# Moving activation loads and spills from ScalarE's DMA queue to GpSimd's in an FFN-attention-FFN kernel on eight cores

## The chip, the cores and the metric

The kernel runs as one program on all 8 cores of one Trainium2 chip. The metric is the device time in microseconds of the slowest core. The cores share no data: each works on its own 2048 tokens of one of four sequences, and recomputes the tokens at the border that its neighbours own.

## What is computed

The reference is one layer of the "macaron" form over x of shape (4, 4096, 1024), in f32:

```python
x = x + 0.5 * ffn(layernorm(x))
x = x + attention(layernorm(x))
x = x + 0.5 * ffn(layernorm(x))
```

`ffn` is a channel mix over neighbouring tokens with three 1024 by 1024 weights, and `attention` has 16 heads of 64 channels, rotary positions and a window of 128 tokens to each side:

```python
x_prev = shift_by_one_token(x)
xr = mu_r * x + (1 - mu_r) * x_prev
xk = mu_k * x + (1 - mu_k) * x_prev
out = sigmoid(xr @ W_r.T) * (square(relu(xk @ W_k.T)) @ W_v.T)
```

## The kernel before

A core works on 20 tiles of 128 tokens (16 of them are its output, the rest is border). The residual x of a tile is f32, 128 by 1024, or 512 KB; it lives in one of eight slots of `xr_sb` (tile number modulo 8) while a tile is in work, and in the DRAM tensor `xscr` between the stages. The three stages follow one another:

- Stage 1, the first FFN (`emit_ffn_stage(1, ...)`): tiles are loaded from the input, normalised in pairs (two passes of ScalarE with sums, L203 and L206, small VectorE steps, L210 to L217, logarithm and exponential on ScalarE, L226 and L227, and L233 on VectorE), transposed by DMA on SyncE's queue, mixed on VectorE (L332, L337, L342), multiplied by W_r and W_k (L364), by W_v (L396), added to x (L409), and written to `xscr`.
- Attention (`emit_attn_stage`): for tile j it computes q, k and v (`emit_qkv`, matmuls L593, bias L598, evacuation by ScalarE L617, into PSUM banks 0 and 1 in turn), then the LayerNorm of tile j + 1 (`emit_ln2`), the attention core of tile j - 2 (scores L696, exponential L705 on ScalarE, gates L710, values L723), and the output projection of tile j - 3 (`emit_wo`, L776, bias L781, added to x by VectorE at L787). Then the finished x of tile j - 3 is written to `xscr`, and tile j + 5 is loaded into the same slot.
- Stage 4, the second FFN: as stage 1, with a border tile ahead (its LayerNorm and transpose into `lnb`), and 16 tiles that go to `out`.

The weights share one SBUF tensor, `warena`, with four columns of 1024: three for the stage's weights and one for the output projection. At start GpSimd's queue loads it with a cast from f32 to f16. During stage 1 the same queue converts the qkv weights into `wqkv16` in DRAM, and at j == 6 of the attention the FFN weights into `ffn16` (three DMAs named `ffn<-wr`, `<-wk`, `<-wv` in the profile). From there ScalarE's queue brings them into `warena`, three DMAs of 2 MB, at the start of attention (`warena<-wqkv`) and near its end (`warena<-ffn`).

The order of the work is written out by hand. `P.op(queue, build, waits, incs)` puts one instruction into the list of one engine (t, v, a, g, y are TensorE, VectorE, ScalarE, GpSimd and SyncE) with its semaphore waits; each engine runs its list in order. A DMA is an instruction of the engine that issues it, so a wait ahead of a DMA holds up all that is behind it in that engine's list:

```python
    GD = lambda o, i: (lambda g: g.dma_start(o, i))
    AD = lambda o, i: (lambda a: a.dma_start(o, i))
```

Before the change all plain transfers of x are in ScalarE's list: the loads of the three stages, the spills of stage 1 and of attention, and the stores to `out`. Each slot has one semaphore, `sl0` to `sl7`, that both its loads and its spills raise. A load waits for `slot_free` of its slot, which is most often the spill of the tile that was there. The ScalarE instructions that copy q, k and v out of PSUM stand behind these DMAs in the same list.

## Time and profile before

| what | value |
|---|---|
| runs shown | 1617.45 and 1629.7 us, median 1623.58 us |
| the profiled execution's own time | 1623.66 us |
| its span, on core 7, the slowest | 1622.1 us |
| spans of the eight cores | 1595.7 to 1622.1 us |
| busy: TensorE matmul, its weight loads | 961.0 us, 417.9 us |
| busy: VectorE, ScalarE, GpSimd | 613.6 us, 497.0 us, 10.3 us |
| mean granted TensorE clock on core 7 | 0.771 |

No engine is busy for more than 59% of the span. On core 7 stage 1 ends at about 442 us, attention runs from 477 us to 1314 us, and stage 4 from there to the end. The page's chain of work gives TensorE 37% of the span, VectorE 19%, DMAs 17%, and 10% to "issue", which is time for which the profile shows no awaited event. The list of waits and the timeline say more here than the shares do: engines take turns, and what counts is which wait ends last at each turn.

### The profile page before, as it was taken

What the parts mean: (1) busy time and instruction counts of PE and PEld (TensorE: products, weight loads), DVE (VectorE), ACT (ScalarE), POOL (GpSimd) and SP (SyncE); (2) the same over time, 40 slices, a digit from 0 to 9 for tenths busy, and PEclk for the clock granted to TensorE, in tenths of its full rate; (3) what the DMA queues carried; (4) which work ended last, traced back from release to release, by engine and by line L of the source; (5) the groups of instructions that cost most, each with busy time, mean ns of one, the idle gap of its engine ahead of it and who ended that gap; (6) DMA issues with size and microseconds to landing.
All of it is one profiled execution on the core that took longest, in us unless ns stands there. A gap on an engine that the chain in (4) does not pass through costs nothing.

```text
span 1622.1 us, 18620 instructions; the slowest of 8 cores (1595.7 to 1622.1 us)
## 1 busy us (share of the span) xinstructions
PE 961.0 (59%) x4645; PEld 417.9 (26%) x4645; DVE 613.6 (38%) x1674; ACT 497.0 (31%) x1054; POOL 10.3 (1%) x18
## 2 busy tenths in 40 slices
PE   0066732776724346663666667777777636776657
PEld 0022311322301123322233333333333312322223
DVE  1174403445402224323234343434444425445543
ACT  0233310432112224322333333343333322332231
POOL 1000000000000000000000000000000000000000
PEclk9998875888857666775677777777777567888878
DMA  9914495331272342269332222222223552333332
GB/s 159 202 33 111 101 127 103 92 91 52 86 232 45 57 67 53 66 92 138 56 66 66 65 60 52 59 59 53 53 53 53 150 197 48 92 91 78 78 72 72
DMA packets 224372, 141.15 MB, mean 87 GB/s; under 512 B 195472, under 2 KB 197648, under 8 KB 224080
## 3 DMA queue, kind: packets, MB, share of 16 engines
q1 hardware_dynamic: 193088, 48.25, 17.3%
q10 hardware_dynamic: 22224, 69.42, 12.6%
q0 software_dynamic: 8960, 22.29, 10.8%
q8 instruction: 45, 0.74, 0.2%
q14 instruction: 55, 0.45, 0.1%
HBM read 86.47 MB, written 39.85 MB: 78 GB/s over the span
## 4 chain that ended last, share of the span: by engine, by line
PE 37%; DVE 19%; DMA 17%; issue 10%; ACT 8%; SPq 4%; ACTq 2%; DVEq 1%; POOL 0%; POOLq 0%
PE pb L593 12%; DMA ln_fm_s<-ln_tm 7%; PE pb L396 6%; PE pb L776 5%; PE pb L696 5%; SPq L136 4%; DVE xkm_s L342 4%; PE pb L723 3%; PE pb L364 3%; DVE xrm_s L337 3%; DMA kfm_s<-kpre_s 3%; DMA ln2fm_s<-ln_tm 2%; DMA xscr<-xr_sb 2%; PE pb L598 2%; ACT qsq L206 2%
## 5 line engine op out<-in xcount | busy, mean ns | idle before, releaser
L593 PE MATMUL pb<-warena,ln2fm_s 128*128 128x512 f16 x912 | 230.3, 398 | 126.3 <-DMA ln2fm_s<-ln_tm 113.0
L396 PE MATMUL pb<-warena,kfm_s 128*128 128x512 f16 x560 | 158.3, 446 | 166.4 <-DMA kfm_s<-kpre_s 166.4
L696 PE MATMUL pb<-qpl_s,kpl_s 65*128 65x128 f16 x816 | 122.6, 288 | 173.5 <-ACT probsT_s L705 171.6
L364 PE MATMUL pb<-warena,xrm_s 128*128 128x512 f16 x560 | 143.0, 414 | 126.4 <-DVE stats L210 52.9
L630 DVE TENSOR_REDUCE qm_s<-qsq 128x16 f32<-128x1024 f16 x19 | 23.2, 1220 | 350.7 <-ACT qsq L624 350.7
L705 ACT ACTIVATE probsT_s<-pb 128x384 bf16<-128x384 f32 x272 | 131.7, 492 | 61.3 <-PE pb L696 39.7
L593 PEld LDWEIGHTS pb<-warena,ln2fm_s 128*128 128x128 f16 x912 | 82.9, 101 | 243.3 <-issue 169.1
L396 PEld LDWEIGHTS pb<-warena,kfm_s 128*128 128x128 f16 x560 | 60.9, 111 | 260.8 <-issue 216.9
L364 PE MATMUL pb<-warena,xkm_s 128*128 128x512 f16 x560 | 126.6, 379 | 0.0
L374 ACT ACTIVATE r_sb_s<-pb 128x512 f16<-128x512 f32 x70 | 38.7, 596 | 282.1 <-issue 192.8
L710 DVE TENSOR_TENSOR probsT_s<-probsT_s,gates_sb 128x256 bf16<-128x256 bf16 x272 | 77.9, 291 | 102.2 <-ACT probsT_s L705 75.9
L203 ACT ACTIVATE ln_tm<-xr_sb 128x1024 f16<-128x1024 f32 x56 | 59.0, 1054 | 184.2 <-issue 105.6
L696 PEld LDWEIGHTS pb<-qpl_s,kpl_s 65*128 65x128 f16 x816 | 63.3, 117 | 195.1 <-issue 184.7
L364 PEld LDWEIGHTS pb<-warena,xrm_s 128*128 128x128 f16 x560 | 57.6, 105 | 208.2 <-issue 155.5
L723 PE MATMUL pb<-vaug_s,probsT_s 128*128 128x65 f16 x816 | 90.4, 236 | 24.8 <-DVE probsT_s L710 9.6
L617 ACT ACTIVATE qaug_s<-pb 128x512 f16<-128x512 f32 x38 | 21.7, 597 | 250.1 <-PE pb L598 143.7
L776 PE MATMUL pb<-warena,attnfm_s 128*128 128x512 f16 x272 | 91.8, 499 | 1.3 <-DVE xr_sb L787 0.9
L332 DVE TENSOR_TENSOR d_fm_s<-ln_fm_s 128x2048 f16<-128x2048 f16 x18 | 22.2, 1235 | 148.7 <-DMA ln_fm_s<-ln_tm 136.8
L723 PEld LDWEIGHTS pb<-vaug_s,probsT_s 128*128 128x128 bf16 x816 | 55.9, 116 | 67.8 <-issue 63.6
L364 PEld LDWEIGHTS pb<-warena,xkm_s 128*128 128x128 f16 x560 | 54.8, 98 | 66.1
L404 DVE SCALAR_TENSOR_TENSOR t_sb_s<-pb,r_sb_s 128x512 f32<-128x512 f32 x70 | 47.0, 688 | 50.1 <-PE pb L396 50.1
L233 DVE TENSOR_SCALAR ln_tm<-xr_sb,stats 128x1024 f16<-128x1024 f32 x56 | 43.9, 811 | 49.1 <-ACT stats L227 49.1
(80 smaller groups left out, 816.3 us busy)
## 6 DMA issues: line engine op xcount, KB each, us to landing
xscr<-xr_sb ACTq DMA_DIRECT2D x36, 512.0 KB, 2.9
xr_sb<-xscr ACTq DMA_DIRECT2D x36, 512.0 KB, 5.2
xr_sb<-x ACTq DMA_DIRECT2D x20, 512.0 KB, 4.3
out<-xr_sb ACTq DMA_DIRECT2D x16, 512.0 KB, 2.9
wqkv<-wqkv POOLq DMA_DIRECT2D x1, 6144.0 KB, 60.0
warena<-wqkv ACTq DMA_DIRECT2D x3, 2048.0 KB, 19.4
warena<-ffn ACTq DMA_DIRECT2D x3, 2048.0 KB, 16.8
warena<-wr POOLq DMA_DIRECT2D x2, 1024.0 KB, 14.5
```

Of the source, the lines that this page charges most:

```text
L136: YT = lambda o, i: (lambda y: y.dma_start(o, i, transpose=True))
L203: P.op("a", lambda a: a.activation(ln_tm[:, par, :], x_ap, AF.Copy, accum_out=sl(0)), waits=list(waits) + lnT_free[par] + stats_free.pop(s ...
L337: P.op("v", lambda v, c=c, gp=gp, o=o: v.scalar_tensor_tensor(xrm2[:, gp, c, o:o + 256], d_fm[:, c, o:o + 256], negmu[:, c:c + 1], ln_fm[: ...
L342: P.op("v", lambda v, c=c, gp=gp, o=o: v.scalar_tensor_tensor(xkm2[:, gp, c, o:o + 256], d_fm[:, c, o:o + 256], negmu[:, 8 + c:9 + c], ln_ ...
L364: t.matmul(pb[bk][:, :], xm[:, gp, c, 128 * ti:128 * (ti + 1)], warena[:, c, woff + 512 * js:woff + 512 * (js + 1)], start=(c == 0), stop= ...
L396: P.op("t", lambda t, bk=bk, c=c, pp=pp, js=js: t.matmul(pb[bk][:, :], kfm[:, pp, c, :], warena[:, c, 2 * DM + 512 * js:2 * DM + 512 * (js ...
L593: P.op("t", lambda t, bk=bk, c=c, par=par, js=js: t.matmul(pb[bk][:, :], ln2fm[:, par, c, :], warena[:, c, 512 * js:512 * (js + 1)], start ...
L696: P.op("t", lambda t, sl=sl, h=h, ci=ci, par=par, bk=bk_sc: t.matmul(pb[bk][:, ci * 128:(ci + 1) * 128], AP(kpl, sl * NH * 128 + h * 128, ...
L705: P.op("a", lambda a, h=h, bk=bk_sc, hp=hp: a.activation(probsT[:, hp, :], pb[bk][:, 0:384], AF.Exp), waits=[("t", sc_tok[(i, h)])] + wp, ...
L710: P.op("v", lambda v, hp=hp, gi=gi: v.tensor_tensor(AP(probsT, hp * 384, [[4 * 384, 128], [256, 2], [1, 128]]), AP(probsT, hp * 384, [[4 * ...
L723: P.op("t", lambda t, sl=sl, h=h, ci=ci, hp=hp, bk=bk_pv: t.matmul(pb[bk][:, 0:65], AP(probsT, hp * 384 + ci * 128, [[4 * 384, 128], [1, 1 ...
L776: P.op("t", lambda t, bk=bk, c=c, par=par, js=js: t.matmul(pb[bk][:, :], attnfm[:, par, c, :], warena[:, c, 3 * DM + 512 * js:3 * DM + 512 ...
```

## The change

The diff has three parts.

1. The loads of x in attention and in stage 4, and the spills of x in attention, go to GpSimd's list, with semaphores of their own for each slot, `gl0` to `gl7`. Stage 1's loads and spills, and the stores to `out`, stay in ScalarE's list on `sl0` to `sl7`. That is 19 loads and 17 spills in attention and 17 loads in stage 4, 53 DMAs.
2. The three loads of the qkv weights get a semaphore each (`awq0` to `awq2`), and a projection waits only for its own third.
3. The two loads of W_r at the start get a semaphore each (`gw0a`, `gw0b`), and each half of the output columns waits for its own.

```diff
--- before.py
+++ after.py
@@ -124,9 +124,10 @@
     pb = [st.enter_context(nc.psum_tensor(f"pb{i}", [128, 512], F32)) for i in range(8)]
 
     P = Prog(nc)
-    STREAMS = (["am", "aw", "aw4r", "aw4k", "aw4v", "ylb"] +
-               [f"sl{i}" for i in range(8)] +
-               ["yl0", "yl1", "yk0", "yk1", "yt0", "yt1", "yt2", "yt3", "yaf0", "yaf1"])
+    STREAMS = (["am", "awq0", "awq1", "awq2", "aw4r", "aw4k", "aw4v", "ylb"] +
+               [f"sl{i}" for i in range(8)] + [f"gl{i}" for i in range(8)] +
+               ["yl0", "yl1", "yk0", "yk1", "yt0", "yt1", "yt2", "yt3", "yaf0", "yaf1",
+                "gw0a", "gw0b"])
     for s in (["g", "a", "y", "t", "v", "s", "ft", "fv", "fa", "fg", "fy",
                "gm", "gw0", "gw1", "gw2", "gwo", "gq6", "gf6"] + STREAMS):
         P.add(s)
@@ -139,11 +140,11 @@
     lnT_free = {0: [], 1: []}
 
     g_ffnw3 = []
-    for hf in range(2):
+    for hf, snw in ((0, "gw0a"), (1, "gw0b")):
         P.op("g", GD(warena[:, :, 512 * hf:512 * (hf + 1)],
                      AP(wr_d.tensor, 512 * hf, [[DM, 128], [128 * DM, 8], [1, 512]])),
-             incs=[("gw0", 16)])
-    g_ffnw3.append(("gw0", P.n("gw0")))
+             incs=[(snw, 16)])
+    g_ffnw3.append([("gw0a", 16), ("gw0b", 16)])
     for o, i in ((wqkvb_sb[:, :], wqkvb_d), (wob_sb[:, :], wob_d), (C_sb[:, :, :], cos_d),
                  (S_sb[:, :, :], sin_d), (pm1_sb[:, :], pm1_d)):
         P.op("g", GD(o, i), incs=[("gm", 16)])
@@ -271,14 +272,17 @@
         kfm_free = {0: [], 1: []}
         rkt_free = {0: [], 1: []}
 
+        qd, pfx = ("a", "sl") if stage == 1 else ("g", "gl")
+
         def load_x(tl):
-            sn = f"sl{tl % 8}"
+            sn = f"{pfx}{tl % 8}"
             w = ([slot_free[tl % 8]] if tl % 8 in slot_free else list(barrier))
             if P.n(sn) > 0:
                 w.append((sn, P.n(sn)))
             if spill_prev is not None and spill_prev.get(tl):
                 w.append(spill_prev[tl])
-            P.op("a", AD(xr_sb[:, tl % 8, :], src[tl * 128:(tl + 1) * 128, :]),
+            P.op(qd, (AD if qd == "a" else GD)(xr_sb[:, tl % 8, :],
+                                               src[tl * 128:(tl + 1) * 128, :]),
                  waits=w, incs=[(sn, 16)])
             xtok[tl] = (sn, P.n(sn))
 
@@ -358,8 +362,9 @@
                 gw = g_w[0] if which == "r" else g_w[1]
                 for js in range(2):
                     bk = bank0 + js
+                    gwj = gw[js] if isinstance(gw, list) else gw
                     for c in range(8):
-                        w = ([("v", mix_tok[(gi, ti // 2)]), gw] + bank_free[bk]) if c == 0 else []
+                        w = ([("v", mix_tok[(gi, ti // 2)]), gwj] + bank_free[bk]) if c == 0 else []
                         P.op("t", lambda t, bk=bk, c=c, ti=ti, js=js, xm=xm, woff=woff, gp=gp:
                              t.matmul(pb[bk][:, :],
                                       xm[:, gp, c, 128 * ti:128 * (ti + 1)],
@@ -549,23 +554,25 @@
         sc_tok = {}
         t_qkv_last = [0]
         def load_x(tl):
-            sn = f"sl{tl % 8}"
+            sn = f"gl{tl % 8}"
             w = [slot_free[tl % 8]] if tl % 8 in slot_free else list(barrier)
             if P.n(sn) > 0:
                 w.append((sn, P.n(sn)))
-            P.op("a", AD(xr_sb[:, tl % 8, :], xscr[tl * 128:(tl + 1) * 128, :]),
+            P.op("g", GD(xr_sb[:, tl % 8, :], xscr[tl * 128:(tl + 1) * 128, :]),
                  waits=w, incs=[(sn, 16)])
             xtok[tl] = (sn, P.n(sn))
 
         for tl in range(1, 6):
             load_x(tl)
+        g_qkv = []
         for part, wkey in ((0, "r"), (1, "k"), (2, "v")):
+            snq = f"awq{part}"
             P.op("a", AD(AP(warena, part * DM,
                             [[8 * 4 * DM, 128], [4 * DM, 8], [1, DM]]),
                  AP(wqkv16.tensor, part * DM,
                     [[3 * DM, 128], [128 * 3 * DM, 8], [1, DM]])),
-                 waits=[("t", t_s1.get(wkey, t_s1_mm)), g_qkv16], incs=[("aw", 16)])
-        g_qkv = ("aw", P.n("aw"))
+                 waits=[("t", t_s1.get(wkey, t_s1_mm)), g_qkv16], incs=[(snq, 16)])
+            g_qkv.append((snq, P.n(snq)))
 
         y_ln2 = {}
 
@@ -589,7 +596,7 @@
             for js in range(6):
                 bk = js % 2
                 for c in range(8):
-                    wm = ([y_ln, g_qkv] + bank_free[bk]) if c == 0 else []
+                    wm = ([y_ln, g_qkv[js // 2]] + bank_free[bk]) if c == 0 else []
                     P.op("t", lambda t, bk=bk, c=c, par=par, js=js: t.matmul(
                         pb[bk][:, :], ln2fm[:, par, c, :],
                         warena[:, c, 512 * js:512 * (js + 1)],
@@ -792,13 +799,13 @@
                     waits=[("t", t_wo), ("v", ln2_tok[i])], incs=[("v", 1)])
                 bank_free[bk] = [("v", P.n("v"))]
             x2_tok = P.n("v")
-            sn = f"sl{i % 8}"
+            sn = f"gl{i % 8}"
             fw = [(sn, P.n(sn))] if P.n(sn) > 0 else []
             if STAGES == 3 and OT0 <= i <= OT1:
-                P.op("a", AD(out_d[(i - OT0) * 128:(i - OT0 + 1) * 128, :], xr_sb[:, i % 8, :]),
+                P.op("g", GD(out_d[(i - OT0) * 128:(i - OT0 + 1) * 128, :], xr_sb[:, i % 8, :]),
                      waits=[("v", x2_tok)] + fw, incs=[(sn, 16)])
             else:
-                P.op("a", AD(xscr[i * 128:(i + 1) * 128, :], xr_sb[:, i % 8, :]),
+                P.op("g", GD(xscr[i * 128:(i + 1) * 128, :], xr_sb[:, i % 8, :]),
                      waits=[("v", x2_tok)] + fw, incs=[(sn, 16)])
             slot_free[i % 8] = (sn, P.n(sn))
             wo_spill[i] = (sn, P.n(sn))
```

The instructions of TensorE, VectorE and SyncE stand in the same order as before; only ScalarE's and GpSimd's lists move. Line numbers of the changed kernel are up to 7 higher (L136 is L135, L204 is L203, L624 is L617, L712 is L705).

The first place is the end of stage 1 on ScalarE. The `xscr<-xr_sb` rows are the last spills, `warena<-wqkv` the weights of attention, L203 the first LayerNorm of attention. Before:

```order
L135 DMA xscr<-xr_sb 128x1024 [waits v,sl2]
L135 DMA xscr<-xr_sb 128x1024 [waits v,sl3]
L135 DMA xr_sb<-xscr 128x1024 [waits sl1]
L135 DMA xr_sb<-xscr 128x1024 [waits sl2]
L135 DMA xr_sb<-xscr 128x1024 [waits sl3]
L135 DMA xr_sb<-xscr 128x1024 [waits sl4]
L135 DMA xr_sb<-xscr 128x1024 [waits sl5]
L135 DMA warena<-wqkv 128x8x1024 [waits t,gq6] x3
L203 ACTIVATE ln_tm,stats<-xr_sb 128x1024 [waits sl1,yl1,v]
```

After:

```order
L136 DMA xscr<-xr_sb 128x1024 [waits v,sl2]
L136 DMA xscr<-xr_sb 128x1024 [waits v,sl3]
L136 DMA warena<-wqkv 128x8x1024 [waits t,gq6] x3
L204 ACTIVATE ln_tm,stats<-xr_sb 128x1024 [waits gl1,yl1,v]
L207 ACTIVATE qsq,stats<-xr_sb 128x1024 [waits s]
L227 ACTIVATE stats<-stats 128x1 [waits v]
L228 ACTIVATE stats<-stats 128x1 [waits s]
```

The five loads are gone from between the last spill and the weights; they now stand in GpSimd's list, and the LayerNorm waits for `gl1` instead of `sl1`.

The second place is the end of one tile in attention (tile 2 on ScalarE before). L733 copies the last head out of PSUM, and L617 copies the next tile's q and k. Before, on ScalarE:

```order
L733 ACTIVATE attn_un_s<-pb 128x65 [waits t]
L135 DMA xscr<-xr_sb 128x1024 [waits v,sl2]
L135 DMA xr_sb<-xscr 128x1024 [waits sl2]
L617 ACTIVATE qaug_s<-pb 128x8x64 [waits t,yt1] x2
L617 ACTIVATE kaug_s<-pb 128x8x64 [waits t,v,yt1] x2
```

After, on GpSimd, from that tile's spill on, with the three conversions of the FFN weights that stood there before too:

```order
L135 DMA xscr<-xr_sb 128x1024 [waits v,gl2]
L135 DMA xr_sb<-xscr 128x1024 [waits gl2]
L135 DMA xscr<-xr_sb 128x1024 [waits v,gl3]
L135 DMA ffn<-wr 1024x1024 [waits t]
L135 DMA ffn<-wk 1024x1024
L135 DMA ffn<-wv 1024x1024
L135 DMA xr_sb<-xscr 128x1024 [waits gl3]
```

The spill and the load have left ScalarE, so L617 follows L733 directly; on GpSimd a load stands behind the spill that it waits for, and one load stands behind the three conversions.

The third place is the end of attention on ScalarE, with the FFN weights of stage 4. Before:

```order
L705 ACTIVATE probsT_s<-pb 128x384 [waits t]
L733 ACTIVATE attn_un_s<-pb 128x65 [waits t]
L135 DMA xscr<-xr_sb 128x1024 [waits v,sl0]
L135 DMA warena<-ffn 128x8x1024 [waits t,gf6]
L135 DMA warena<-ffn 128x8x1024 x2
L705 ACTIVATE probsT_s<-pb 128x384 [waits t] x3
```

After:

```order
L712 ACTIVATE probsT_s<-pb 128x384 [waits t]
L740 ACTIVATE attn_un_s<-pb 128x65 [waits t]
L136 DMA warena<-ffn 128x8x1024 [waits t,gf6]
L136 DMA warena<-ffn 128x8x1024 x2
L712 ACTIVATE probsT_s<-pb 128x384 [waits t] x3
```

The spill of tile 16, which waits for VectorE's sum, stood ahead of the weights before, and no longer does.

## Rows read from the trace of the kernel before

**Rows 1.** Waits of the whole span: engine, line, waited for, us in total, times, longest.

```profile
ACT qaug_s L617 <- DMA xscr<-xr_sb: 106.4, 9, 17.3
PE pb L593 <- ACT qaug_s L617: 13.3, 9, 7.7
PE pb L364 <- DVE stats L210: 52.9, 1, 52.9
```

**Rows 2.** Timeline around one usual tile: start us, us, engine, line [idle before].

```profile
820.44 0.33 ACTq L135 DMA_DIRECT2D xscr<-xr_sb  x1
821.20 0.38 PE L598 MATMUL pb<-wqkvb_sb,ones 1*128 1x512 f16 x1
...
823.68 1.09 ACT L617 ACTIVATE qaug_s<-pb 128x512 f16<-128x512 f32 x2 [11.46 <-DMA xscr<-xr_sb]
...
824.42 1.89 PE L593 MATMUL pb<-warena,ln2fm_s 128*128 128x512 f16 x8 [0.68 <-ACT qaug_s L617]
```

**Rows 3.** Timeline, the tile beside the conversion of the FFN weights.

```profile
701.14 0.69 DVE L787 TENSOR_TENSOR xr_sb<-pb,xr_sb 128x512 f32<-128x512 f32 x1 [1.46 <-PE pb L781]
701.52 0.77 POOL L134 DMA_DIRECT2D ffn<-wr  x1 [502.67 <-PE pb L781]
...
713.01 3.57 PE L593 MATMUL pb<-warena,ln2fm_s 128*128 128x512 f16 x8 [7.74 <-ACT qaug_s L617]
```

**Rows 4.** Timeline, the same tile's transposes on SP and the next projection.

```profile
730.89 21.55 SPq L136 DMA_TRANSPOSE qpl_s<-qaug_s  x1
...
752.58 15.51 SPq L136 DMA_TRANSPOSE kpl_s<-kaug_s  x1
...
775.19 3.57 PE L593 MATMUL pb<-warena,ln2fm_s 128*128 128x512 f16 x8 [22.87 <-DMA ln2fm_s<-ln_tm]
```

**Rows 5.** Timeline, from the first stage to attention.

```profile
444.97 4.15 ACTq L135 DMA_DIRECT2D xr_sb<-xscr  x5
...
449.26 9.12 ACTq L135 DMA_DIRECT2D warena<-wqkv  x3
...
458.60 1.06 ACT L203 ACTIVATE ln_tm<-xr_sb 128x1024 f16<-128x1024 f32 x1 [24.39 <-issue]
...
464.83 1.34 SPq L136 DMA_TRANSPOSE ln2fm_s<-ln_tm  x1
...
476.77 3.24 PE L593 MATMUL pb<-warena,ln2fm_s 128*128 128x512 f16 x8 [34.52 <-DMA ln2fm_s<-ln_tm]
```

**Rows 6.** Windows of that stretch: busy us by engine, clock, DMA share, GB/s.

```profile
455.00:460.00 5.00, 0.00 (x0) 0.00 (x0) 0.00 (x0) 1.40 (x3) 0.00 (x0) 0.50 0.96 281
```

**Rows 7.** Timeline, the last three tiles of attention.

```profile
1279.90 0.51 PE L696 MATMUL pb<-qpl_s,kpl_s 65*128 65x128 f16 x6
...
1281.80 6.96 ACTq L135 DMA_DIRECT2D warena<-ffn  x3
1288.92 0.88 ACT L705 ACTIVATE probsT_s<-pb 128x384 bf16<-128x384 f32 x2 [16.12 <-issue]
```

**Rows 8.** Timeline, from attention to the last stage.

```profile
1313.84 0.34 ACTq L135 DMA_DIRECT2D xscr<-xr_sb  x1
...
1321.34 1.06 ACT L203 ACTIVATE ln_tm<-xr_sb 128x1024 f16<-128x1024 f32 x1 [20.63 <-DMA xr_sb<-xscr]
```

**Rows 9.** Timeline of ACT in the last stage, with a load and without.

```profile
1411.07 0.34 ACTq L135 DMA_DIRECT2D out<-xr_sb  x1
...
1412.43 1.06 ACT L203 ACTIVATE ln_tm<-xr_sb 128x1024 f16<-128x1024 f32 x1 [7.75 <-issue]
...
1552.17 0.34 ACTq L135 DMA_DIRECT2D out<-xr_sb  x1
1552.73 1.06 ACT L203 ACTIVATE ln_tm<-xr_sb 128x1024 f16<-128x1024 f32 x1 [6.33 <-DVE xr_sb L409]
```

**Rows 10.** Source line of the POOL DMAs: count, ns min/median/max, first and last.

```profile
L134 POOL DMA_DIRECT2D C_sb<-cosx x1: 593/593/593, 4.5 to 4.5; - x1
```

**Rows 11.** Instructions on xr_sb: ns min/median/max.

```profile
L787 DVE TENSOR_TENSOR xr_sb<-pb,xr_sb x34: 685/692/693, 657.1 to 1313.0; 128x512 f32<-128x512 f32 x34
```

## The prediction

> **What bounds the kernel now.** Read the page's first two parts first: no engine is busy for 60% of the span, so the time is set by waits at the turns between engines. The page's chain has three kinds of turn that a DMA queue can touch, and the list of waits and the timeline price them.
>
> The list of waits shows ScalarE waiting 106.4 us, in 9 pieces, for the spill `xscr<-xr_sb` ahead of the copy of q [rows 1]. That number is not what the wait costs. Of the 11.46 us of one such piece [rows 2] ScalarE had no work anyway until TensorE had finished the first group of the projection, at 821.20 + 0.38 = 821.58. The spill was issued at 820.44 and had to land, and the load behind it had to be issued, before the copy at 823.68. TensorE lost only the 0.68 us before its third group at 824.42, since it has two banks to fill first. The same list gives the sum of that loss: 13.3 us in 9 pieces, the longest 7.7 [rows 1].
>
> The two other turns are between the stages. Into attention, ScalarE's list holds five loads, three weight loads and only then the LayerNorm, and TensorE stands still for 34.52 us [rows 5]. Out of attention, three weight loads stand behind the spill of tile 16, and the exponentials behind these [rows 7].
>
> The sum is made against the profiled execution's own 1623.66 us; the median of the runs shown, 1623.58, is the same for this purpose.
>
> **Usual tiles.** Without spill and load in its list ScalarE can copy at 821.6 and is done before TensorE's second group ends, so the 0.68 goes; what is late next is TensorE itself. Eight of the nine pieces are of this kind: 13.3 - 7.7 = 5.6 us. They lie on the path, since everything behind in the tile (norm of q, LayerNorm, exponentials) starts from the last group. Bounds: 5 and 6.
>
> **The tile beside the conversions.** Here the spill landed late, and TensorE lost 7.74 us [rows 3]. But the next steps are transposes, and these crawl while GpSimd's three conversions fill the DMA engines: they hold SP's queue for 21.55 and 15.51 us, and TensorE then waits 22.87 us, until 775.19, for a transpose behind them [rows 4]. The conversions start with the same matmul as before, so their end doesn't move, and a transpose that starts 7.7 us earlier only crawls longer. I take 2 us of the 7.7; bounds 0 and 7.7.
>
> **Into attention.** ScalarE starts its five loads at 444.97 and its weights at 449.26. The loads leave the list, so the weights start 4.3 us earlier, and with them the LayerNorm (458.60) and its transpose (464.83). The transpose then took until 476.77, almost 12 us, in a stretch where the DMA engines are 0.96 busy at 281 GB/s [rows 5, 6]. GpSimd's list changes what is in that stretch: tile 1's load (its slot is free since tile 17's spill) and tile 2's go out before it, but tiles 6 to 8, which ScalarE issued later, between the first projections, are now issued at once. That is one load of 0.52 MB more, 0.52 / 0.281 = 1.9 us of transfer. 4.3 - 1.9 = 2.4, and I take 2.5. Bounds: if the weights of ScalarE's queue share the engines with six loads at once, the third weight DMA, whose issue already blocks (three take 9.12 us), blocks for longer and the LayerNorm comes up to 4 us late; if the transposes also run faster, 6 us are won.
>
> **The semaphore per third, and per half of W_r.** Nothing: TensorE at 476.77 waited for the transpose, not for weights [rows 5]; at the start it waits 52.9 us for VectorE's statistics [rows 1], with W_r issued at the very start. The cover of the first is gone only if the last third lands more than four groups after the first.
>
> **Out of attention.** TensorE has the scores of the last core's first heads at 1279.90 + 0.51 = 1280.41, but ScalarE issues the FFN weights from 1281.80, which takes 6.96 us, and the first exponential is at 1288.92. ScalarE had been idle since 1288.92 - 16.12 = 1272.80, waiting for the spill's turn [rows 7]. Without that spill in its list the weights go out at 1272.80, are issued at 1279.8, and the exponential comes at 1280.5: 8.4 us, all on the path, since the last core and two output projections follow. Next late is TensorE's own chain. Bounds: 8.5, and 4, if the weights now slow the transpose of tile 17's attention that is needed some 12 us later.
>
> **Into stage 4.** The last spill and the load behind it now pass through GpSimd. Before, 1321.34 - 1313.84 = 7.5 us pass from the spill's issue to the LayerNorm [rows 8]. Issuing 512 KB takes GpSimd 0.59 us [rows 10] where ScalarE needs 0.34 [rows 8]: 0.5 us for both. No row shows how long an unhindered transfer of GpSimd takes; I charge 1 us in all, near the one known part, with bounds of 1 us won and 6 lost (each transfer twice as long).
>
> The Trainium skill ("DMA: Bandwidth & Descriptors", section on the anatomy of one DMA on the gpsimd path) gives about 2.0 us plus the bytes over 436 GB/s for such a DMA, an estimate of 3.2 us for 512 KB, so 6.4 for two. By it this term would be a gain of 1.1 us and the sum 1601. No run here shows it.
>
> **Inside stage 4.** The stores stay and the loads leave. From a store to the LayerNorm behind it pass 1412.43 - 1411.07 = 1.36 us with a load between and 0.56 without [rows 9], so up to 0.8 us for each of the five pairs of tiles that have a load there, 4.0 in all; the issue alone is 0.33, 1.7 in all. I take 3. The LayerNorm is on the path there (its transposes and the mix release the next matmuls).
>
> **What GpSimd's list can delay.** The load of tile 11, the spill of tile 4 and the load of tile 12 now stand behind the conversions. These are over by 775.19, 74 us after 701.52 [rows 3, 4], while attention spends 44 us on a tile (19 tiles in 837 us) and tile 11 is needed four tiles later. Hidden, with 100 us to spare. The 53 issues of 0.33 us that leave ScalarE, 17.5 us, are otherwise in its idle time.
>
> **The sum.** 5.6 + 2 + 2.5 + 8.4 - 1 + 3 = 20.5 us. 1623.66 - 20.5 = 1603.2, which I give as 1603, 1.3% faster. A measurement of this kernel can tell about 2% from no change, which is 32.5 us.
>
> **The rivals.**
>
> First, everything at its better bound: 6 + 7.7 + 6 + 8.5 + 1 + 4 = 33 us, 1590. For it speaks that ScalarE and the transposes get rid of competing transfers in the crowded stretches; against it, that the conversions and the weights are as long as before. Chance 0.2.
>
> Second, the new turns are worse than the old: the six loads beside the weights cost the 2.5 us and 4 more, and the last spill and load cost 6 instead of 1. 20.5 - 6.5 - 5 = 9 us gained, 1615. For it: the engines are full at that turn [rows 6]. Chance 0.2.
>
> Third, slower: GpSimd and VectorE block each other. GpSimd is occupied for 0.59 us by each DMA; if each of the 53 held VectorE on the path for that long, 31.3 us, the result is 1603.2 + 31.3 = 1634. It decides from 20.5 / 53 = 0.39 us each. Against it: VectorE's add at 701.14 ran into GpSimd's issue at 701.52 and took 0.69 us [rows 3], as all 34 of its kind do, 685 to 693 ns [rows 11]; and VectorE is idle when a usual tile's spill is issued. For it: this add reads PSUM, so it says little of others. Chance 0.06.
>
> A rule of the Trainium skill speaks for this rival ("SBUF — State Buffer", section on who interferes with whom): GpSimd shares a pair of SBUF ports with VectorE under an exclusive lock, descriptors of GpSimd's DMAs are written through it, and single-source VectorE operations in their fast modes take it too. No row here has both at once in such a mode.
>
> Fourth, the moved waits come back under another name (a LayerNorm waiting for its load in place of a copy waiting for a spill), and the time stays at 1624. The five tiles between load and use speak against it. Chance 0.04.
>
> **How the numbers follow.** The forecast has 0.5, the four rivals 0.2, 0.2, 0.06 and 0.04. The range for 8 in 10 takes in the first rival's end nearly and the second: 1591 to 1617. More than 2% faster is 1591.1 or less: half of the first rival and a little of the forecast's edge, from a sum of small terms that I may have missed, 0.17. More than 2% slower is 1656, which needs 1 us of VectorE for each of the 53: 0.03. Within 2%: 0.8.
>
> **What would show it right or wrong.** Right: no wait of the copy of q (L617, now L624) for `xscr<-xr_sb`; TensorE's wait for that copy gone; the first exponential of the last core within 1 us of its scores; the first projection of attention 2 to 3 us sooner after stage 1; 1 us more from the last sum to stage 4's first LayerNorm. Wrong: the tile beside the conversions passing its 7.7 us on to the next projection; TensorE standing longer than 34.5 us before attention; VectorE operations longer than before, or a LayerNorm waiting for `xr_sb<-xscr` inside attention.

## The result, and the profile after

| | before | after |
|---|---|---|
| median of the runs | 1625.88 us (10 runs) | 1605.89 us (11 runs) |
| the profiled execution | 1623.66 us | 1602.91 us |
| spans of the eight cores | 1595.7 to 1622.1 us | 1588.5 to 1601.4 us |

The ratio of after to before is 0.9887, with a 95% interval of 0.9863 to 0.991: 1.1% faster, inside the band of 2% and 3 us from the forecast of 1603. In some executions of either kernel the cores of one die run longer at a lower granted clock; the medians contain these, the ratio doesn't. The total came out near the forecast; several of its terms did not, one loss at the very end was missing, and, as the table shows, the total owes a part to luck.

The page of the changed kernel, of core 2, its slowest: the busy times.

```profile
PE 945.7 (59%) x4645; PEld 414.1 (26%) x4645; DVE 613.6 (38%) x1674; ACT 496.7 (31%) x1054; POOL 38.4 (2%) x71
```

GpSimd's count of instructions grew by the 53 moved DMAs, from 18 to 71, and VectorE is busy for the same 613.6 us as before. The list of waits of the whole span (engine, line, waited for: us in total, times, longest):

```profile
POOL xscr L135 <- DVE xr_sb L794: 715.0, 16, 188.3
POOL xr_sb L135 <- DMA xscr<-xr_sb: 305.3, 14, 230.5
ACT qaug_s L624 <- PE pb L605: 239.5, 38, 40.7
PE pb L600 <- DMA ln2fm_s<-ln_tm: 111.5, 5, 36.5
```

The first row of [rows 1], ScalarE's copy of q waiting for a spill, is gone: the copy now waits for TensorE in all 38 of its pieces. The second row of [rows 1], TensorE waiting for that copy, has no successor in the list. The spill and the load wait on GpSimd instead. What that delays there is the start of the conversions, and the end of the program; both come below.

Shares say little about where 20 us went, so I cut the span at events that both kernels have, all on VectorE but the last, and took the mean over the eight cores: the last add of stage 1, the norm of q of each tile j of attention, the last sum of attention (L787), the border tile's row (L296), the adds of stage 4, and the last instruction of all. A mean over cores also evens out the span's spread of 26 us between cores.

| stretch | before | after | difference | forecast |
|---|---|---|---|---|
| to the last add of stage 1 | 446.3 | 444.6 | -1.7 | 0 |
| to the first norm of q | 51.2 | 51.4 | +0.2 | -2.5 |
| tiles 1 to 5 | 134.2 | 127.9 | -6.3 | 0 |
| tile 5 to 6 | 42.6 | 42.0 | -0.6 | -0.7 |
| tile 6 to 7 (late spill) | 49.0 | 41.7 | -7.3 | with the next: -2 |
| tile 7 to 8 (conversions) | 63.3 | 71.9 | +8.6 | |
| tiles 8 to 15 | 297.3 | 290.9 | -6.4 | -4.9 |
| tiles 15 to 19 | 165.6 | 164.7 | -0.9 | 0 |
| to the last sum of attention | 56.8 | 49.5 | -7.3 | -8.4 |
| to the border tile's row | 18.3 | 20.9 | +2.6 | +1 |
| to the first add of stage 4 | 43.4 | 43.4 | 0 | |
| stage 4, first add to last | 234.8 | 234.6 | -0.2 | -3 |
| together, to the last add of stage 4 | 1602.9 | 1583.5 | -19.4 | -20.5 |
| from there to the last instruction | 6.8 | 11.3 | +4.5 | 0 |
| whole span, mean of the eight cores | 1609.8 | 1594.8 | -14.9 | -20.5 |

Stage 1 of before and of the kernels below scatters from 443.7 to 446.4 us in the same way wherever its code is the same, so its -1.7 belongs to no edit.

The last two rows matter for the verdict on the sum. The mean over the cores fell by 14.9 us, the slowest core of the two profiled executions by 20.7 (1622.1 to 1601.4), because it stood 12.3 us above the mean before and 6.6 after. Nothing in the forecast was about that spread, so this part of the agreement is luck.

**The end of the program.** The last add of stage 4 is followed by its store. Then GpSimd, which waits for all others, runs the DRAIN instruction that closes its list. Its row in the views of L859 and L866 (count, ns min/median/max, first and last start), before first:

```profile
L859 POOLq DRAIN  x1: 1203/1203/1203, 1620.3 to 1620.3; - x1
```

```profile
L866 POOLq DRAIN  x1: 5450/5450/5450, 1595.7 to 1595.7; - x1
```

It is 4.25 us longer on each of the eight cores, and it grows with the number of DMAs that GpSimd has issued: 1.20 us with 14, 4.14 with 50 (experiment 6), 5.45 with 67, 6.18 with 76 (experiment 8), 6.67 with 82 (experiment 9), 7.41 with 91 (experiment 10). That is 0.08 us for each DMA, paid once, at the end.

**A usual tile.** The timeline of after where [rows 2] stood: start us, us, engine, line, with the idle time before in brackets.

```profile
810.36 0.54 POOL L135 DMA_DIRECT2D xscr<-xr_sb  x1 [46.59 <-DVE xr_sb L794]
810.65 0.39 PE L605 MATMUL pb<-wqkvb_sb,ones 1*128 1x512 f16 x1
811.18 0.60 ACT L624 ACTIVATE qaug_s<-pb 128x512 f16<-128x512 f32 x1 [8.96 <-PE pb L605]
813.12 1.90 PE L600 MATMUL pb<-warena,ln2fm_s 128*128 128x512 f16 x8
814.03 0.53 POOL L135 DMA_DIRECT2D xr_sb<-xscr  x1 [3.14 <-DMA xscr<-xr_sb]
```

The copy starts 0.14 us after the bias matmul and not 2.1 us, and the third group has no idle time before it.

**The tile beside the conversions.** SyncE's transposes in after, of q of the tile before (its k took 2.37 us), and then of the tile itself:

```profile
671.49 1.97 SPq L137 DMA_TRANSPOSE qpl_s<-qaug_s  x1
...
713.06 22.07 SPq L137 DMA_TRANSPOSE qpl_s<-qaug_s  x1
735.28 24.40 SPq L137 DMA_TRANSPOSE kpl_s<-kaug_s  x1
759.88 2.70 SPq L137 DMA_TRANSPOSE ln2fm_s<-ln_tm  x1
```

Those of q and k hold the queue for 46.5 us; they held it for 37.1 in [rows 4]. The copy of q is on time now, its transposes come sooner under the conversions, and crawl longer. The windows of that stretch (PE, PEld, DVE, ACT and POOL busy, granted clock, DMA share, GB/s):

```profile
720.00:740.00 20.00, 13.10 (x87) 7.00 (x87) 8.88 (x39) 6.10 (x17) 0.54 (x1) 0.67 1.04 121
740.00:760.00 20.00, 0.00 (x0) 0.00 (x0) 0.00 (x0) 0.00 (x0) 0.00 (x0) 0.50 1.05 155
```

For 20 us no engine works at all; the DMA engines are full, and move only 121 to 155 GB/s.

As a mean over the cores, the three conversions have landed 61.4 us after their start before and 61.5 us after, and the transpose of k ends 0.8 and 1.1 us behind them. But they start later: 2.0 us after the matmul that releases them and not 0.55, since the spill, which waits for VectorE's sum, now stands ahead of them in GpSimd's list.

**Into attention.** The timeline where [rows 5] stood:

```profile
447.95 9.75 ACTq L136 DMA_DIRECT2D warena<-wqkv  x3
453.86 3.12 POOL L135 DMA_DIRECT2D xr_sb<-xscr  x6 [6.73 <-DMA xscr<-xr_sb]
457.92 1.06 ACT L204 ACTIVATE ln_tm<-xr_sb 128x1024 f16<-128x1024 f32 x1 [20.80 <-issue]
464.14 1.36 SPq L137 DMA_TRANSPOSE ln2fm_s<-ln_tm  x1
481.69 3.57 PE L600 MATMUL pb<-warena,ln2fm_s 128*128 128x512 f16 x8 [36.46 <-DMA ln2fm_s<-ln_tm]
```

Since stage 1 ends at another time on each core, I took this turn from the last add of stage 1, as a mean over the cores. The weights' issue starts after 1.8 us (6.0 before), and the LayerNorm after 11.4 (16.7): 5.3 us sooner. The transpose behind it then takes 17.0 us to its landing, and took 11.4: it runs beside six loads, of tiles 2 to 7, that GpSimd issued at once, on this core from 453.86. The first projection starts after 34.6 us, and started after 34.3.

The weights land later too. Of the three `warena<-wqkv` on this core:

```profile
DMA to landing us min/median/max: 15.0/30.3/34.6
```

The third was issued at 449.9 and so landed at 484.5, 2.8 us after the first matmul of 481.69 had begun. As a mean over the cores it lands 37.4 us after the last add of stage 1, 2.8 us behind the first matmul; before it landed at 33.7, 0.6 us ahead of it.

**Out of attention and into stage 4.**

```profile
1254.98 5.95 ACTq L136 DMA_DIRECT2D warena<-ffn  x3
1262.19 0.51 PE L703 MATMUL pb<-qpl_s,kpl_s 65*128 65x128 f16 x6
1262.69 0.87 ACT L712 ACTIVATE probsT_s<-pb 128x384 bf16<-128x384 f32 x2 [7.61 <-PE pb L703]
...
1288.89 0.53 POOL L135 DMA_DIRECT2D xscr<-xr_sb  x1 [3.89 <-DVE xr_sb L794]
1292.76 4.79 POOL L135 DMA_DIRECT2D xr_sb<-xscr  x8 [3.34 <-DMA xscr<-xr_sb]
1298.01 1.06 ACT L204 ACTIVATE ln_tm<-xr_sb 128x1024 f16<-128x1024 f32 x1 [23.83 <-DMA xr_sb<-xscr]
```

The last core's first exponential follows its scores at once; in [rows 7] it came 8.5 us after them. From the last spill's issue to stage 4's first LayerNorm pass 1298.01 - 1288.89 = 9.1 us, and 7.5 in [rows 8].

### The profile page after: what moved, and what is told of

Read it like the earlier page. It is cut to its first block, busy times and chain, and to the rows that moved or that the text cites. A ratio compares the mean times of both kernels' runs of the same rounds, so it can differ in the third digit from the quotient of the medians.

```text
span 1601.4 us, 18625 instructions; the slowest of 8 cores (1588.5 to 1601.4 us)
## 1 busy us (share of the span) xinstructions
PE 945.7 (59%) x4645; PEld 414.1 (26%) x4645; DVE 613.6 (38%) x1674; ACT 496.7 (31%) x1054; POOL 38.4 (2%) x71
## 4 chain that ended last, share of the span: by engine, by line
PE 39%; DVE 19%; DMA 17%; issue 10%; ACT 8%; SPq 5%; ACTq 2%; DVEq 1%; POOL 0%; POOLq 0%
PE pb L600 14%; DMA ln_fm_s<-ln_tm 7%; PE pb L401 6%; PE pb L783 5%; PE pb L703 5%; SPq L137 4%; DVE xkm_s L346 4%; PE pb L730 3%; DMA kfm_s<-kpre_s 3%; DVE xrm_s L341 3%; PE pb L369 3%; PE pb L605 2%; ACT qsq L207 2%; DMA ln2fm_s<-ln_tm 2%; DMA pm_sb<-pm 2%
## 5 line engine op out<-in xcount | busy, mean ns | idle before, releaser
L369 PE MATMUL pb<-warena,xrm_s 128*128 128x512 f16 x560 | 136.8, 401 | 128.7 <-DVE stats L211 53.1
L712 ACT ACTIVATE probsT_s<-pb 128x384 bf16<-128x384 f32 x272 | 131.3, 490 | 52.7 <-PE pb L703 46.6
L369 PE MATMUL pb<-warena,xkm_s 128*128 128x512 f16 x560 | 126.6, 379 | 0.0
L204 ACT ACTIVATE ln_tm<-xr_sb 128x1024 f16<-128x1024 f32 x56 | 58.9, 1052 | 190.2 <-issue 62.2
L369 PEld LDWEIGHTS pb<-warena,xrm_s 128*128 128x128 f16 x560 | 56.1, 102 | 205.7 <-issue 149.5
L624 ACT ACTIVATE qaug_s<-pb 128x512 f16<-128x512 f32 x38 | 22.7, 597 | 239.5 <-PE pb L605 239.5
L336 DVE TENSOR_TENSOR d_fm_s<-ln_fm_s 128x2048 f16<-128x2048 f16 x18 | 22.2, 1234 | 146.1 <-DMA ln_fm_s<-ln_tm 136.3
L369 PEld LDWEIGHTS pb<-warena,xkm_s 128*128 128x128 f16 x560 | 54.8, 98 | 66.1
```

The costliest lines, as they stand in the source:

```text
L204: P.op("a", lambda a: a.activation(ln_tm[:, par, :], x_ap, AF.Copy, accum_out=sl(0)), waits=list(waits) + lnT_free[par] + stats_free.pop(s ...
L369: t.matmul(pb[bk][:, :], xm[:, gp, c, 128 * ti:128 * (ti + 1)], warena[:, c, woff + 512 * js:woff + 512 * (js + 1)], start=(c == 0), stop= ...
L712: P.op("a", lambda a, h=h, bk=bk_sc, hp=hp: a.activation(probsT[:, hp, :], pb[bk][:, 0:384], AF.Exp), waits=[("t", sc_tok[(i, h)])] + wp, ...
```

## The experiments

Ten kernels were timed, each beside the kernel before on the same chip. Its median was 1626.24 us beside experiments 1, 3, 4 and 6, 1620.39 beside 2, 5, 7 and 8, and 1618.46 beside 9 and 10, so ratios compare across them and times don't. The stretches are the same means over eight cores, each from one profiled execution. Most single edits are worth less than the whole times can tell apart, so the stretches carry the argument.

**1. The weights ahead of the spill of tile 16.** From before, `emit_wo(16)` and the block of the FFN weights change places:

```diff
+            if j == NT - 1:
+                for sn4, i in (("aw4r", 0), ("aw4k", 1), ("aw4v", 2)):
+                    P.op("a", AD(warena[...], ffn16[...]), ...)
             if QT0 <= j - 3 <= QT1:
                 emit_wo(j - 3)
```

> The kernel before with one move: ScalarE's three DMAs of the stage-4 weights stand ahead of the output projection and spill of tile 16, all x transfers stay on ScalarE. If the order in ScalarE's list is what mattered at the end of attention, the stretch from tile 19's norm sum to the last projection sum shortens by about 7 us (56.8 before, 49.6 in the changed kernel) and nothing else moves: about 0.45% faster. If it was the transfers' queue that mattered, the stretch stays at 56 to 57 us.

Measured: 1622.82 us, ratio 0.999 (0.9963 to 1.0018). The stretch to the last sum fell from 56.8 to 53.8 us, not to 50. ScalarE's timeline on core 3:

```profile
1275.26 2.34 ACTq L135 DMA_DIRECT2D warena<-ffn  x3
...
1283.88 4.25 ACTq L135 DMA_DIRECT2D xscr<-xr_sb  x1
1288.29 0.88 ACT L705 ACTIVATE probsT_s<-pb 128x384 bf16<-128x384 f32 x2 [12.93 <-issue]
```

The weights are issued in 2.34 us, but the spill behind them takes 4.25 us to issue, where a usual one takes 0.33 [rows 2], and the exponential waits for it. Over the eight cores this issue takes 1.7 to 5.7 us, 3.3 as a mean. So the order explains three of the seven us, and most of the rest is that a DMA issued behind 6 MB on the same queue blocks its engine.

**2. That spill alone on GpSimd.** From before:

```diff
+                if i == 16:
+                    sn = "gx"
+                    P.op("g", GD(xscr[i * 128:(i + 1) * 128, :], xr_sb[:, i % 8, :]), ...)
```

> The kernel before with one transfer moved: the spill of tile 16 goes to GpSimd's list, so that the three loads of the FFN weights stand behind no spill in ScalarE's list. The order of the earlier run, weights first and the spill behind them, left the spill's issue blocked for 3 to 4 us. My theory: the whole 7 us of the changed kernel out of attention come from this one transfer: the stretch from the last norm of q to the last sum of attention falls from 56.8 to 49.5 us (that run had 53.8), 1619 us. The rival, that the changed kernel's gain there comes from all spills and loads being away from the ring of the weights: 53 to 54 us as in that run, 1623 us.

Measured: 1614.04 us, ratio 0.9939 (0.989 to 0.9988). The stretch is 49.6 us, the changed kernel's 49.5, and the others are within 1.5 us of before, apart from stages 1 and 4, which scatter (see below). One transfer of 53 carries all of this term.

**3. The load one projection later.** From before, all on ScalarE; from tile 10 on, a load is issued behind the next projection's copies, when its spill has long landed:

```diff
-                load_x(j + 5)
+                if j < 5:
+                    load_x(j + 5)
+                else:
+                    pending_load.append(j + 5)
...
             emit_qkv(j)
             if j + 1 < NT:
                 emit_ln2(j + 1)
+            while pending_load:
+                load_x(pending_load.pop(0))
```

> The kernel before with the reload of a slot in attention issued by ScalarE one projection later, so that its spill has long landed; nothing goes to GpSimd. If the wait for the landing ahead of the copy of q is what the move to GpSimd took away, the stretches from tile 5 to tile 15 shorten as in the changed kernel: 0.7 us a usual tile, 7 us for the tile beside the conversions, of which the next tile gives back most; sum about 6 to 8 us. If GpSimd's queue itself was what helped (its transfers disturb the transposes less), these stretches stay within 2 us of before.

Measured: 1617.41 us, ratio 0.9966 (0.9927 to 1.0005). Tile 6 to 7 is 41.6 us and tiles 8 to 15 take 291.6, within 0.7 us of after, with no transfer of x on GpSimd. So nearly all of the 0.9 us per usual tile was the wait for the spill's landing and not ScalarE's two issues of 0.33. Tile 7 to 8 is 65.8, between before (63.3) and after (71.9); its stage 4 is 239.1, which I take up below.

**4. The loads of tiles 6 to 8 as late as before.** From after:

```diff
+            if 6 <= tl <= 8:
+                w.append(("s", P.n("s")))
```

> The changed kernel, with the loads of tiles 6 to 8 held back on GpSimd until ScalarE's list is where it issued them before. Theory: in the changed kernel these three loads run beside the qkv weights; that costs the entry into attention about 2.5 us (51.4 us there, expected 49 here) and saves the tiles 1 to 5 about 6 us, because before they ran beside the transposes of the LayerNorm (127.9 us there, expected 134 here, as before the change). So this kernel should be 3 to 4 us slower than the changed one. Rival: tiles 1 to 5 got shorter by ScalarE's issues leaving; then they stay at 128 and this kernel is as fast or faster.

Measured: 1607.77 us, ratio 0.9897 (0.9876 to 0.9918). The first norm of q comes 47.9 us after stage 1 (51.4 in after), and tiles 1 to 5 take 136.8 (127.9). Both halves of what the three early loads do are there: they cost 3.5 us beside the weights, and save 8.9 later, more than was expected. The whole time (0.9897 against the changed kernel's 0.9887) doesn't tell the two kernels apart. Where they save it, the transposes of `ln2fm` in tiles 2 to 5 show (landing us, min/median/max); before first, then after, on core 3:

```profile
DMA to landing us min/median/max: 3.2/5.9/8.2
```

```profile
DMA to landing us min/median/max: 2.7/3.2/3.4
```

In before, ScalarE's loads of tiles 6 to 8 ran beside them. The four landings add up, as a mean over the cores, to 20.1 us in before, 12.2 in after, 22.2 here and 12.2 in experiment 5.

**5. The same loads held only until the first projection has begun.** From after:

```diff
+            if 6 <= tl <= 8:
+                w.append(("t", t_first[0]))
```

where `t_first` is the end of the first group of projection 1.

> The changed kernel, with the loads of tiles 6, 7 and 8 held on GpSimd until the first group of the first projection is done: behind the weights, but ahead of where ScalarE's list had them. My theory: they cost 3.5 us when they lie beside the weights and 6 to 9 us when they lie beside the first tiles' transposes; here they land in the first projection, so the first norm of q comes 48 us after stage 1's last add (51.4 in the changed kernel) and tiles 1 to 5 take 128 to 130 us: 1603 us. The rival, that it is the place behind the weights itself that slows tiles 1 to 5, whoever of them releases the loads: 48 and 136 us, 1608 us, as in the run that held them longer.

Measured: 1594.29 us, ratio 0.9828 (0.978 to 0.9876). The first norm of q comes 46.9 us after stage 1, and tiles 1 to 5 take 127.6. TensorE's first wait of attention:

```profile
465.47 1.35 SPq L137 DMA_TRANSPOSE ln2fm_s<-ln_tm  x1
477.44 3.57 PE L605 MATMUL pb<-warena,ln2fm_s 128*128 128x512 f16 x8 [32.91 <-DMA ln2fm_s<-ln_tm]
482.09 2.17 POOL L135 DMA_DIRECT2D xr_sb<-xscr  x4 [29.42 <-PE pb L610]
```

The transpose takes 12.0 us here, and 12.7 as a mean over the cores, where it took 17.0. The rival, that the place behind the weights itself slows tiles 1 to 5, falls. By the ratios this kernel is some 9 us faster than the changed one, while its stretches differ by 4.4; where the rest lies is not shown.

**6. Stage 4's loads back on ScalarE.** From after, `qd, pfx = ("a", "sl")` for both FFN stages.

> The changed kernel with stage 4's loads back on ScalarE; attention's loads and spills stay on GpSimd. Theory: inside stage 4 nothing was won by moving the loads, since TensorE reaches the next group of matmuls earlier but runs it longer at the lower clock, so the stage stays at 234 to 235 us and the time is that of the changed kernel within 1 us plus or minus; the gap from the last sum to the border tile's row falls from 20.9 by about 1 us, as one of the two transfers is ScalarE's again. Rival (the prediction's term): 3 us slower inside stage 4.

Measured: 1606.56 us, ratio 0.9888 (0.986 to 0.9915), the changed kernel's own ratio. Stage 4 takes 235.3 us (234.6 in after, 234.8 in before), and the border tile's row comes after 19.6 us (20.9 in after), as expected. The LayerNorm behind a store is in fact later with a load between, here in this kernel:

```profile
1422.12 0.34 ACTq L136 DMA_DIRECT2D out<-xr_sb  x1
1422.66 0.33 ACTq L136 DMA_DIRECT2D xr_sb<-xscr  x1
1423.20 1.06 ACT L204 ACTIVATE ln_tm<-xr_sb 128x1024 f16<-128x1024 f32 x1 [7.15 <-issue]
```

and in after without one:

```profile
1424.31 0.34 ACTq L136 DMA_DIRECT2D out<-xr_sb  x1
1424.86 1.06 ACT L204 ACTIVATE ln_tm<-xr_sb 128x1024 f16<-128x1024 f32 x1 [7.31 <-DVE xr_sb L414]
```

1.08 us against 0.55. So the 17 moved loads start the LayerNorm 0.5 us sooner in five pairs, and the stage is no shorter. The end of the program is 1.3 us shorter than in after, with 17 DMAs fewer on GpSimd.

**7. The semaphores alone.** From before, one semaphore for each third of the qkv weights and each half of W_r, as in the change.

> The kernel before with the new semaphores alone: one for each third of the qkv weights and one for each half of W_r; all transfers of x stay in ScalarE's list. My theory: nothing, since TensorE waited there for a transpose and at the start for VectorE's statistics: 1626 us on this chip, every stretch within 0.5 us of before (first norm of q 51.2 us after stage 1's last add). The rival, that part of what the change won in tiles 1 to 5 comes from the semaphores: those tiles 128 us in place of 134, and 1620 us.

Measured: 1623.4 us, ratio 1.0017 (0.9992 to 1.0043); the first norm of q after 50.2 us, tiles 1 to 5 in 134.6 (before 134.2). Tile 6 to 7 is 50.2, 1.2 over before. In the kernel before the semaphores are worth nothing.

**8. The FFN conversions in pieces.** From after:

```diff
-            if j == 6:
-                for ii, wd in enumerate((wr_d, wk_d, wv_d)):
-                    P.op("g", GD(ffn16[:, ii * DM:(ii + 1) * DM], wd), ...)
+            if 6 <= j < 18:
+                ii, rr = divmod(j - 6, 4)
+                wd = (wr_d, wk_d, wv_d)[ii]
+                P.op("g", GD(ffn16[256 * rr:256 * (rr + 1), ii * DM:(ii + 1) * DM],
+                             wd[256 * rr:256 * (rr + 1), :]),
+                     waits=[("t", sc_tok[(j - 2, 3)])], incs=[("gf6", 16)])
```

> The changed kernel, with the three conversions of the FFN weights cut into 12 pieces of 256 rows, one in each of tiles 6 to 17, each released by the scores of that tile's fourth head. My theory: the tile beside the conversions is slow because these fill the DMA engines for some 60 us and the transposes crawl; in pieces each is over before the next transposes, and the step from the norm of q of tile 7 to that of tile 8 falls from 71.9 to 43 us, the others stay within 1 us of 41.6: 29 us less, some 1577 us against 1606. The rival, that the work of the conversions only spreads: 12 tiles each 2 us or more longer, 1600 us or more.

Measured: 1571.32 us, ratio 0.9679 (0.9625 to 0.9734). Tile 7 to 8 takes 41.2 us (71.9), tiles 8 to 15 take 290.2 (290.9), tiles 15 to 19 163.9 (164.7). The work does not spread. By the ratios it is 2.1% faster than the changed kernel. A piece, and the next transposes of q and of `ln2fm`, 35 us and more behind it:

```profile
681.35 0.57 POOL L135 DMA_DIRECT2D ffn<-wr  x1 [20.12 <-PE pb L703]
```

```profile
717.10 2.03 SPq L137 DMA_TRANSPOSE qpl_s<-qaug_s  x1
...
721.71 1.73 SPq L137 DMA_TRANSPOSE ln2fm_s<-ln_tm  x1
```

The median piece lands after 5.8 to 6.6 us by core, the slowest after 8.2, long before them.

**9. The qkv conversion in pieces.** From after, the one DMA of 6 MB into `wqkv16` becomes 16 DMAs of 64 rows, in GpSimd's list, one or two for each tile of the second to fourth group, each waiting for that tile's first matmuls (L369).

> The changed kernel, with the one conversion of the qkv weights in stage 1 cut into 16 pieces of 64 rows, one or two in each tile of the second to fourth group, each released by that tile's first matmuls. My theory, the same as for the FFN weights: in stage 1 one pair of tiles takes 71.6 us in place of 25 to 26 beside that conversion, because a transpose into ln_fm crawls for 44 us; in pieces that pair falls to 26 us and the others grow by less than 1 us each: the last add of stage 1 at 402 us in place of 444.6, and 1563 us. The rival, that the pieces reach the transposes of every pair, since a pair has only 34 us: each of six pairs 4 us or more longer, and 1580 us or more.

Measured: 1560.96 us, ratio 0.9665 (0.9626 to 0.9703). By the ratios it is 2.2% faster than the changed kernel. Stage 1's last add is at 401.7 us (444.6). On core 2 the steps between its adds were, in after, 24.9, 9.5, 71.6, 8.2 and 24.9 us around the conversion, and are 24.9, 9.4, 26.1, 8.4 and 26.2. SyncE's transposes into `ln_fm` there, after first, then this kernel:

```profile
180.58 2.71 SPq L137 DMA_TRANSPOSE ln_fm_s<-ln_tm  x2
193.55 8.41 SPq L137 DMA_TRANSPOSE kfm_s<-kpre_s  x2
216.76 44.28 SPq L137 DMA_TRANSPOSE ln_fm_s<-ln_tm  x2
```

```profile
178.52 2.71 SPq L137 DMA_TRANSPOSE ln_fm_s<-ln_tm  x2
191.50 8.15 SPq L137 DMA_TRANSPOSE kfm_s<-kpre_s  x2
213.58 2.72 SPq L137 DMA_TRANSPOSE ln_fm_s<-ln_tm  x2
```

**10. All three together.** After with the edits of 5, 8 and 9.

> The changed kernel with both conversions in pieces and the loads of tiles 6 to 8 held until the first projection has begun. My theory: the three act at different places and add up: 1606 us less 34 (FFN pieces), less 42 (qkv pieces), less 5 (held loads): 1525 us, ratio 0.94 to the kernel before. The rival, that the 8 cores share what the conversions used to hold back and something else binds: 1540 us or more.

Measured: 1533.13 us, ratio 0.948 (0.9447 to 0.9514), 5.2% faster than before, and by the two ratios (0.948 / 0.9887) 4.1% faster than the changed kernel. The stretches are those of the single edits: 46.5 us to the first norm of q, 127.4 for tiles 1 to 5, 41.1 for tile 7 to 8. Stage 1 ends at 404.8 us, 3 later than with the pieces alone, though its code is the same; that and the rest of the miss of 8 us I haven't traced.

## Why the prediction was right, and where its steps were not

The sum was 20.5 us. As a mean over the cores 19.4 were won up to the last add of stage 4, 1.7 of them by scatter in stage 1, and 4.5 were lost again behind it. That the measured time still meets the forecast is luck in two places: a gain that the sum did not have, in tiles 1 to 5, paid for the terms that failed, and the slowest core gained more than the mean did.

**Usual tiles: forecast 5.6, measured 7.9** (the steps 5 to 6 and 8 to 19; all but the last four have a load). The mechanism is the one named, since moving only the load's place (experiment 3) gives 291.6 us for tiles 8 to 15, where after has 290.9 and before 297.3. The size comes out at 7.0 / 8 = 0.88 us for each tile with a load, against the 0.7 that the list of waits gives.

**The tile beside the conversions: forecast 2 won, measured 1.3 lost.** The step before it won 7.3 as read from [rows 3], and the next gave back 8.6. So the sign of being wrong came true: the tile passed its gain on to the next step, and more. The argument, that a transpose which starts sooner under the conversions crawls longer, held, and fully: the transpose of k ends with the conversions in both kernels, so nothing of the 7.7 us was left. The step that failed is "The conversions start with the same matmul as before, so their end doesn't move": in GpSimd's list they now stand behind the spill, start 1.45 us later after that matmul, and take as long. That is the size of the 1.3 lost, though no run moved their place alone. With the spill and the load on ScalarE (experiment 3) the conversions start as early as before, and the two steps together take 107.4 us, 4.9 less than before; there the load is also out of the way of the transposes, and how much each of the two gives is open. Experiment 8 shows what the sum had taken as given: without the long conversions the two steps take 82.9 us, so some 30 us of this kernel lay there, more than in all the terms of the sum together.

**Into attention: forecast 2.5, measured 0.** The first half held: the weights start 4.2 us sooner and the LayerNorm 5.3. The step that failed is "that is one load of 0.52 MB more, 0.52 / 0.281 = 1.9 us of transfer": the transpose lands 5.6 us later. The three loads that used to come after it cost 3.5 to 4.5 us (51.4 against 47.9 and 46.9 us in experiments 4 and 5), 1.2 to 1.5 us each, so the price of one was not too low; the count was. I had set tiles 1 and 2 off against tiles 6 to 8, but only tile 1's load goes out before the weights; tile 2's is the first of the six. The second rival named just this, and this half of it came true. On the slowest cores TensorE stands idle for 36.46 us and not 34.52, a sign of being wrong that the prediction had named (as a mean over the cores, 35.5 and 35.2).

**Tiles 1 to 5: forecast nothing, measured 6.3 won.** This term was missing, and it is what paid for the ones that failed. I had followed the loads of tiles 6 to 8 to where they went, and not asked what they had stood beside before: the transposes of `ln2fm`, whose landing fell from a median of 5.9 us to 3.2 on core 3. In experiment 4 the term goes away together with the early loads, and in experiment 7 it isn't there.

**The semaphores: forecast 0, measured 0 in the kernel before (experiment 7), but not in the changed one.** The reason given, that TensorE waits for the transpose and not for weights, holds before, where the last third lands 0.6 us ahead of the first matmul. In after, beside six loads, it lands 2.8 us behind it, and the single semaphore of before would have held all projections for it. So without the second part of the diff the entry would by this trace have lost about 3 us instead of nothing; no run took the semaphores out of the changed kernel. That the third is needed only after four groups, as the prediction says, is what makes them cover it.

**Out of attention: forecast 8.4, measured 7.3.** The first exponential came at once behind its scores, as forecast. The missing 1.1 us come from reading the wait on core 7 alone: there the exponential came 8.5 us after its scores, and as a mean over the eight cores 7.4. Experiment 2 shows that one spill carries the term, and experiment 1 that it must leave the queue of the weights, and not only its place in the order.

**Into stage 4: forecast 1 lost, measured 2.6.** As means over the cores: GpSimd issues the last spill 0.5 us later after its sum than ScalarE did, and the way from that issue to the LayerNorm is 0.6 us longer (8.0 and 7.4 us; the 9.1 us of core 2 above is the longest). That is the 1 us of the forecast. The spill lands after 2.9 us where ScalarE's took 2.6, and the first of the eight loads, the border tile's, after 4.2 where it took 3.8. From the transfers of the whole span (KB each, median us from issue to landing), before first, where the spills took 2.9, then after:

```profile
lnb_s<-ln_tm SPq DMA_TRANSPOSE x1, 4.7
```

```profile
xscr<-xr_sb POOLq DMA_DIRECT2D x17, 512.0 KB, 3.1
lnb_s<-ln_tm SPq DMA_TRANSPOSE x1, 8.0
```

The rest is the border tile's transpose, which lands after 8.0 us on core 2 and not 4.7 as on core 7; as means over the cores 6.5 and 4.7. This step the term had left out. The last of the eight loads lands 19.8 us after the last sum of attention and not 17.3, and the transpose lands 0.9 us behind it, before and after; that these loads hold it up is inferred, not tested. The Trainium skill ("DMA: Bandwidth & Descriptors", the anatomy of one DMA on the gpsimd path) had given an estimate of 3.2 us for 512 KB. The spills' median of 3.1 us agrees with it; the load that the path hangs on is the first of eight in a row and took 4.2, and with the issues the two took 8.0 us and not 6.4, so the term was a loss and not the gain that the page's figure gave.

**Inside stage 4: forecast 3, measured 0.2 to 0.7** (experiment 6). The LayerNorm does start 0.5 us sooner. The step that failed is that it "is on the path": TensorE's wait for the transpose of `kpre`, in the list of waits of this stage, before and after, was

```profile
PE pb L396 <- DMA kfm_s<-kpre_s: 57.6, 8, 10.9
```

```profile
PE pb L401 <- DMA kfm_s<-kpre_s: 64.8, 8, 11.0
```

so 7.2 us more of waiting stand there in after on these two cores, and 5.0 as a mean over the eight, counted from the stage's first add (60.0 and 55.0). The pace is the same: three windows of 34 us from 1380 us hold 96 matmuls each in after, and 96, 95 and 97 in before, at a granted clock of 0.85 in all six. What closes a pair's loop, so that an earlier LayerNorm doesn't shorten it, isn't settled by these runs. This stage also scatters, from 232.0 to 239.1 us in kernels whose stage 4 is the same as before, so a term of 3 us is at the edge of what its mean tells.

**The end of the program: forecast nothing, measured 4.5 lost.** The sum had no term for it, and what GpSimd's list can delay was asked only for the load of tile 11. The closing DRAIN of GpSimd is 4.25 us longer with 53 DMAs more, on every core, behind the last work of all others.

**The rivals.** The third, GpSimd blocking VectorE, falls. The instructions on `xr_sb` in after (ns min/median/max), beside [rows 11]; the first took 805/812/815 before:

```profile
L234 DVE TENSOR_SCALAR ln_tm<-xr_sb,stats x56: 806/812/815, 54.5 to 1538.3; 128x1024 f16<-128x1024 f32 x56
L794 DVE TENSOR_TENSOR xr_sb<-pb,xr_sb x34: 683/692/693, 650.0 to 1287.6; 128x512 f32<-128x512 f32 x34
```

No operation on it got longer, and all of VectorE is busy for 613.6 us in both. The lock on the shared port of the Trainium skill ("SBUF — State Buffer", who interferes with whom) may exist, but 53 more DMAs from GpSimd took nothing measurable from VectorE here. The fourth, waits under another name, falls too: no LayerNorm inside attention waits for a load. Of the second the half at the entry came true, and the half at the exit at 2.6 of 6 us. The first, everything at its best, had a gain in the same places where the forecast had one and none was found.

## What to carry to other kernels

When a transfer is moved, price both places: what it runs beside now, and what it ran beside before; here the second was worth 6.3 us and had not been asked. Look, too, at what now stands behind it in the new list (the conversions, 1.45 us) and at what the new engine has to do at the end (0.08 us per DMA, 4.25 in all). Moving a DMA off an engine that must do something soon paid where its wait held up that engine (0.9 us per tile, 7 us at the one spill), and nothing where only its issue of 0.33 us went. And before counting half microseconds, look for the stretch in which the DMA engines are full and all others idle: cutting two bulk conversions into pieces that fit between the transposes shortened their stretches by 31 and 43 us, with the same bytes moved. A sum that meets the gain of the slowest core should still be set against the mean over the cores: here 20.7 and 14.9 us.

## What the runs showed of the hardware

- A DMA's issue isn't a fixed cost. On ScalarE's queue it takes 0.33 us for a usual spill, but 1.7 to 5.7 behind three loads of 2 MB (experiment 1, eight cores), and those three take 2.34 us to issue in experiment 1 and 9.75 in after by what else is under way. The engine stands for that time.
- Transposes by DMA take some ten times as long beside a DRAM-to-DRAM conversion: 22 and 24 us where 2 are usual, with the DMA engines at 1.04 and 1.05 and only 121 and 155 GB/s, and 44 us in stage 1 where two take 2.7, at 1.00 and 1.02 and 119 and 145 GB/s. Conversions in pieces of 384 and 512 KB that end before the transposes leave them at their usual time (experiments 8 and 9).
- GpSimd takes 0.53 us to issue a transfer of 512 KB, ScalarE 0.33; as medians over the span its spills land about alike, after 3.1 and 2.9 us.
- GpSimd's DRAIN at the end of the program takes 1.20 us after 14 DMAs and 5.45 after 67, 0.08 us for each, in all kernels measured here.
